# Two key tiles per step in both attention layers of a two-layer transformer kernel

## What is computed

```python
def _layernorm(x, axis=-1, eps=1e-05):
    m = jnp.mean(x, axis=axis, keepdims=True)
    v = jnp.var(x, axis=axis, keepdims=True)
    return (x - m) / jnp.sqrt(v + eps)
...
q_hk = (hidden_q @ Wq.T).reshape(Bv, Sv, H, K)            # H, K = 16, 128
q_big = jnp.einsum('bshk,hkq->bshq', q_hk, w_kc_q)        # layer 0 rotates q_big too
kv_r = _apply_rope(kv_c, sin_k[None], cos_k[None])
q_r = jnp.einsum('bshq,hqr->bhsr', q_big, W_qr)
k_r = jnp.einsum('bld,hdr->bhlr', kv_r, W_kr)
attn = jax.nn.softmax(jnp.einsum('bhsr,bhlr->bhsl', q_r, k_r), axis=-1)
ctx_c = jnp.einsum('bhsl,bld->bhsd', attn, kv_r)
ctx_lat = jnp.einsum('bhsd,hkd->bhsk', ctx_c, w_kc_kv)
return ctx_lat.transpose(0, 2, 1, 3).reshape(Bv, Sv, H * K) @ Wo.T
...
x = x + _L0_xattn_ref(_layernorm(x), ctx_512, ...)
x = x + _L0_ffn_ref(_layernorm(x), ...)                   # 16 experts
x = x + _L1_xattn_ref(_layernorm(x), ctx_512, ...)
x = x + _L1_ffn_ref(_layernorm(x), ...)                   # LoRA experts
```

## Time and profile before

| | us |
|---|---|
| median of 3 runs | 3165.96 (3162.75 to 3173.43) |
| the profiled execution | 3168.89 |
| its span, first to last instruction | 3167.1 |
| layer 0's attention, 192 to 1431 of the span | 1239, PE busy 1142.5 |
| layer 1's attention, 1849 to 2822 | 973, PE busy 938.5 |
| the rest (weights, experts, LoRA experts) | 955, PE busy 772.3 |

### The profile page before, as it was taken

The page is one execution under the profiler, slowest core; times in us unless marked ns, Lnnn a source line. Parts: engine busy times, 40 slices in busy tenths (PEclk is TensorE's granted clock), DMA queues, the critical chain, the costliest instruction groups (busy, mean ns, idle before and its releaser), DMA issues. The chain is left out here.

```text
span 3167.1 us, 42548 instructions
## 1 busy us (share of the span) xinstructions
PE 2853.3 (90%) x15928; PEld 1633.2 (52%) x15928; DVE 1954.6 (62%) x2322; ACT 1177.4 (37%) x1640; POOL 1668.3 (53%) x935
## 2 busy tenths in 40 slices
PE   7689899999998999996899889999999999986898
PEld 6444444444544454443788744444454454445665
DVE  2576667666766676655666556655665655636664
ACT  2124441444144423442333234444443443433331
POOL 0467775776677776771200047677676666742111
PEclk8689999999999999997899989999999999997998
DMA  8333331333133322322000143232323232300000
GB/s 288 109 84 75 87 92 34 88 76 104 36 76 84 92 58 62 75 52 85 1 1 1 28 89 80 66 78 63 75 63 75 63 75 63 83 30 23 7 6 12
DMA packets 98836, 209.15 MB, mean 66 GB/s; under 512 B 30306, under 2 KB 74322, under 8 KB 91116
## 3 DMA queue, kind: packets, MB, share of 16 engines
q1 hardware_dynamic: 98636, 206.44, 25.1%
HBM read 135.36 MB, written 46.00 MB: 57 GB/s over the span
## 5 line engine op out<-in xcount | busy, mean ns | idle before, releaser
L1135 POOL TENSOR_TENSOR sums<-sums,prob 125x896 f32<-125x896 f32 x556 | 1176.1, 2115 | 285.2 <-ACT prob L1075 242.2
L1222 DVE TENSOR_REDUCE maxpart<-pair 112x2 f32<-112x1000 f32 x744 | 889.9, 1196 | 451.8 <-PE pair L937 451.3
L1075 ACT ACTIVATE prob<-wide 125x896 f32<-125x896 f32 x768 | 704.4, 917 | 903.0 <-PE wide L963 901.1
L977 PE MATMUL single<-prob,kv 125*64 125x448 f32 x3072 | 753.8, 569 | 0.5
L958 PE MATMUL wide<-qhigh,kparts 64*125 64x448 f32 x3072 | 448.7, 369 | 1.5 <-DVE maxpart L1222 1.5
L937 PE MATMUL pair<-kparts,qhigh 64*112 64x500 f32 x1488 | 360.7, 481 | 88.0 <-DVE maxpart L1222 86.5
L937 PEld LDWEIGHTS pair<-kparts,qhigh 64*112 64x112 f32 x1488 | 130.1, 171 | 520.6 <-DVE maxpart L1222 440.0
L1135 POOL TENSOR_TENSOR sums<-prob 125x896 f32<-125x896 f32 x64 | 135.1, 2111 | 362.2 <-ACT prob L1075 362.2
L958 PEld LDWEIGHTS wide<-qhigh,kparts 64*125 64x125 f32 x3072 | 281.7, 184 | 79.6 <-issue 48.2
L963 PE MATMUL wide<-shift,ones_row 64*125 64x448 f32 x1536 | 284.5, 365 | 3.9 <-DMA shift<-maxrow 3.9
L958 PE MATMUL wide<-qlow,kparts 64*125 64x448 f32 x1536 | 283.0, 363 | 0.0
(11 more groups left out here) (329 smaller groups left out, 3898.2 us busy)
## 6 DMA issues: line engine op xcount, KB each, us to landing
...
```

Of the source, the lines that this page charges most:

```text
L977: mm = pe.matmul(mix_acc[64 * half:64 * half + DC, 0:HQ], kv[:, b % 3, t, :], prob[:, (b * LT + t) % NPROB, half * HQ:(half + 1) * HQ], st ...
L1075: nc.scalar.activation(prob[:, n_ % NPROB, :].rearrange("p (a b) -> p a b", a=2), acc[0:LP, :, 0:HQ], ACT.Exp)\
L1135: nc.gpsimd.tensor_tensor(dst, first_in, prob[:, n_ % NPROB, :], ALU.add).then_inc(s["pool_sum"], 1)
L1222: V.tensor_reduce(maxpart[:, b % 2, t:NMAX:4, third], acc[0:TQ, :, 0:LB], AX.X, ALU.max).then_inc(*R.signal_drained(kind, *key))
```

## The change

The list is written two tiles at a time. In pair p of a batch (t = 2p) come: maximum t, score t, score t+1, maximum t+1, then mix t-2 and mix t-1, then what falls due. In pair 0 the two mixes are the last ones of the batch before. Other steps move with that:

- `context` of the batch before comes behind pair 0's mixes, so behind both maxima of pair 0; before, it stood ahead of the first of these maxima.
- `spread` (the packed reciprocal) stands in the fourth pair (tiles 6 and 7) instead of tile 8, `share` in the sixth.
- Layer 0: `rope` 0 stands behind the first maximum of pair 1, `rope` 1 behind the second; the three `keyT` end pairs 2, 3 and 4; `ropecos` 0 and 1 stand behind the first maxima of pairs 4 and 5, `rotate` behind the second of pair 4.
- Layer 0, last batch of a group: the two `rstd` stand at the ends of pairs 4 and 5 (before: tiles 7 and 8), `xsplit` at the end of pair 5 (before: tile 9).
- Layer 1: the next group's norm is spread over batches j = 4 and j = 5, with the reciprocal in four pieces (`invert`, 112 columns each) and the products with it in four (`scale`), and the subtraction of `xsplit` in two (`xrest`). Two queries fall in one pair, the first between the maximum and the scores.

```diff
@@ -47,6 +47,8 @@
+NORM_PARTS = (2, 4)
+REST_PARTS = (1, KT)
...
@@ -112,44 +123,60 @@
         maximum(1, i, (PAIR, 0)[i % 2])
     for b in range(NB):
         g, j = divmod(b, BG)
+        following = g + 1 < G
+        for p in range(LT // 2):
+            t = 2 * p
+            queries = following and j == BG - 2 and p < NPAIR // 2
+            if p == 1 and b + 2 < NB:
                 add("fetch", b + 2)
+            ahead(b, t)
+            if queries:
+                add("query", g + 1, t, region=3)
+            if following and j == BG - 4 and p == 3:
+                add("square", g + 1, 0)
+            if following and j == BG - 3 and 1 <= p <= 4:
+                add("scale", g + 1, p - 1)
+            if following and j == BG - 3 and p == 5:
+                add("xrest", g + 1, 0)
+            add("score", b, t, region=0)
+            add("score", b, t + 1, region=1)
+            if b + 1 < NB and p == 4:
                 add("maxneg", b + 1)
+            ahead(b, t + 1)
+            if b + 1 < NB and p == 4:
+                add("maxT", b + 1, region=3)
+            if queries:
+                add("query", g + 1, t + 1, region=3)
+            if p or b:
+                old = (b, t - 2) if p else (b - 1, LT - 2)
+                add("mix", old[0], old[1])
+                add("mix", old[0], old[1] + 1)
+                if not p:
                     add("context", b - 1)
+            if p == 1 and b:
                 add("norm", b - 1, region=3)
+            if g and j == 1 and 2 <= p <= 4:
+                for m, half in (((0, 0),), ((0, 1),), ((1, 0), (1, 1)))[p - 2]:
+                    add("project", g - 1, m, half, region=None if half else 3)
+            if following and j == BG - 4:
+                if p == 2:
                     add("mean", g + 1, region=3)
+                if p == 3:
+                    add("square", g + 1, 1)
+                if p == 5:
                     add("var", g + 1, region=3)
+            if following and j == BG - 3:
+                if p < NORM_PARTS[1]:
+                    add("invert", g + 1, p)
+                if p == 4:
                     add("xsplit", g + 1)
+                if p == 5:
+                    add("xrest", g + 1, 1)
+            if p == 3 and b:
                 add("spread", b - 1)
+            if p == 5 and b:
                 add("share", b - 1, 2)
+    add("mix", NB - 1, LT - 2)
     add("mix", NB - 1, LT - 1)
     add("context", NB - 1)
     add("norm", NB - 1, region=3)
...
@@ -242,59 +270,70 @@
             add("maxT", first, region=3)
             if g:
                 add("attn", g - 1, 3)
-        last = None
         for j in range(BG):
             b = first + j
-            for t in range(LT):
-                ahead = (j + 1, t + EARLY_MAX) if t + EARLY_MAX < LT else (j + 2, t + EARLY_MAX - LT)
-                if layer == 0 and b == 0 and t == 0:
+            for p in range(LT // 2):
+                t = 2 * p
+
+                def ahead(tile):
+                    n = tile + EARLY_MAX
+                    batch, n = (j + 1, n) if n < LT else (j + 2, n - LT)
+                    if batch < BG:
+                        maximum(first + batch, n)
+
+                if b == 0 and p == 0:
                     add("rotate", 2)
                     for part in range(2):
                         add("ropecos", 2, part)
-                if layer == 0 and t == LT - 3 and b + 3 < NB:
+                ahead(t)
+                if p == 1 and b + 2 < NB:
+                    add("rope", b + 2, 0)
+                if p >= 4 and b + 3 < NB:
+                    add("ropecos", b + 3, p - 4)
+                if g + 1 < G and j == BG - 1 and p in (2, 3):
+                    add("square", g + 1, p - 2)
+                add("score", b, t, region=0)
+                add("score", b, t + 1, region=1)
+                if j + 1 < BG and p == 4:
+                    add("maxneg", b + 1)
+                ahead(t + 1)
+                if j + 1 < BG and p == 4:
+                    add("maxT", b + 1, region=3)
+                if p == 4 and b + 3 < NB:
                     add("rotate", b + 3)
-                add("score", b, t, region=t % 2)
-                if j + 1 < BG and t == 8:
-                    add("maxneg", b + 1)
-                if last is not None:
-                    add("mix", *last)
-                    if last[1] == LT - 1:
-                        add("context", last[0])
-                last = (b, t)
-                if t == 1 and j:
-                    add("norm", b - 1, region=3)
-                if j + 1 < BG and t == 9:
-                    add("maxT", b + 1, region=3)
-                if layer == 0 and t in (3, 4, 5) and b + 2 < NB:
-                    add("keyT", b + 2, t - 3, region=3)
-                if layer == 0 and t == LT - 1 and b + 2 < NB:
+                if j or p:
+                    old = (b, t - 2) if p else (b - 1, LT - 2)
+                    add("mix", old[0], old[1])
+                    add("mix", old[0], old[1] + 1)
+                    if not p:
+                        add("context", b - 1)
+                if p == 1:
+                    if j:
+                        add("norm", b - 1, region=3)
+                    if b + 2 < NB:
+                        add("rope", b + 2, 1)
+                if p in (2, 3, 4) and b + 2 < NB:
+                    add("keyT", b + 2, p - 2, region=3)
+                if p == 5 and b + 2 < NB:
                     add("stash", b + 2)
-                if ahead[0] < BG:
-                    maximum(first + ahead[0], ahead[1])
-                if t == 8 and j:
+                if p == 3 and j:
                     add("spread", b - 1)
-                if t == 10 and j:
+                if p == 5 and j:
                     add("share", b - 1, 2)
-                if layer == 0 and t >= LT - 2 and b + 3 < NB:
-                    add("ropecos", b + 3, t - LT + 2)
-                if layer == 0 and t in (1, 2) and b + 2 < NB:
-                    add("rope", b + 2, t - 1)
-                if g + 1 < G and j == BG - 2 and t == 4:
+                if g + 1 < G and j == BG - 2 and p == 2:
                     add("heads", g + 1)
                 if g + 1 < G and j == BG - 1:
-                    if t == 2:
+                    if p == 1:
                         add("mean", g + 1, region=3)
-                    if t in (3, 4):
-                        add("square", g + 1, t - 3)
-                    if t == 5:
+                    if p == 3:
                         add("var", g + 1, region=3)
-                    if t in (7, 8):
-                        add("rstd", g + 1, t - 7)
-                    if t == 9:
+                    if p in (4, 5):
+                        add("rstd", g + 1, p - 4)
+                    if p == 5:
                         add("xsplit", g + 1)
-                    if t == 10:
                         for n in range(SPLIT_AHEAD):
                             add("wsplit", g + 1, n)
+    add("mix", NB - 1, LT - 2)
     add("mix", NB - 1, LT - 1)
     add("context", NB - 1)
     add("norm", NB - 1, region=3)
...
+                elif kind == "invert":
+                    g, part = key
+                    cols = slice(part * NT // norm_parts, (part + 1) * NT // norm_parts)
+                    dve.wait_ge(*R.drained("var", g))
+                    V.reciprocal(x_rstd[:, cols], x_std[:, cols]).then_inc(s["rstd"], 1)
+                elif kind == "scale":
+                    g, part = key
+                    cols = slice(part * NT // norm_parts, (part + 1) * NT // norm_parts)
+                    dve.wait_ge(s["rstd"], norm_parts * g + part + 1)
+                    V.tensor_tensor(x_n[:, :, cols], x_cen[:, :, cols], x_rstd[:, cols].unsqueeze(1).broadcast_to([128, KT, NT // norm_parts]), ALU.mult)\
+                        .then_inc(s["normed"], 1)
+                elif kind == "xrest":
+                    g, k = key
+                    dve.wait_ge(s["x_high"], g + 1)
+                    V.tensor_tensor(x_low[:, k, :], x_n[:, k, :], x_high[:, k, :].bitcast(F32), ALU.subtract).then_inc(s["x_low"], 1)
+                elif kind == "xsplit" and layer == 0:
```

54 lines of the change are left out of this document (17 added, 37 removed).

## The result

The changed kernel takes 3115.77 us (3114.37 to 3117.37, four runs) against 3164.36 for the kernel before in the same comparison: a ratio of 0.984 (95% interval 0.982 to 0.986). The forecast was 3163 with a range down to 3118.

A forecast was written before the change was run, and what follows sets the result against it. PE was taken to set the time wherever nobody makes it wait, with DVE's two-input operations and POOL's additions excluding each other. Layer 0's +36 and layer 1's -39 gave -3 us, so 3163 us against the 3166.0 median; range 3118 to 3187.

The forecast's parts named there:

- (1) *Two tiles per step: Per pair of tiles on PE: 3.90 us against 4.25, by saving one round trip of tile shapes.
- (3) *context: Behind pair 0's maxima, DVE's context waits for POOL's first addition; maximum b of pair 1 starts 1.7 us late.
- context first: Rival, chance 0.05: if POOL's first addition came 0.3 us later, context would cost nothing; 3075 us.
- (4) *keyT: Layer 0, ends of pairs 2 to 4: DVE's subtraction ahead of reduction a costs 0.65 us each, three times.
- (5) *ropecos 0: Layer 0, pair 4: ropecos 0 waits for POOL's addition 7, delaying maxneg; PE waits 1.0 us at maxT (0.4 to 2.3).
- the clock: Rival, chance 0.04: new waits bring a 1.2 GHz stretch in every batch, 64 x 1.7 = 109 us more; 3272 us.
- (6) *ropecos 1: Layer 0, pair 5: POOL's addition 10 is first by 0.08 us, so the next pair starts 1.5 us late.
- ropecos 1 first: Rival, chance 0.27: DVE gets ahead of POOL's addition 10, so 1.5 us falls away in 23 batches; 3128 us.
- The eighth batch: Layer 0, with the query stage: x_low ends about 7 us after PE's last mix; net +3 us (0 to +7).
- Layer 0's +36: Layer 0's total in us: 3 x (7.4 + 3), and +5 in the last group.
- layer 1's sum: Layer 1: eight batches take 239.3 us against 249.3, four times: -39; a regular batch 24.3 + 1.7 = 26.0.
- ctx_n late: Rival, chance 0.14: layer 1's ctx_n misses the gap, waits for addition 10, delays maximum b by 1.9 us; 3175 or 3187.

## Why the prediction was wrong, step by step

The prediction was wrong: the time lies 47 us below it and just outside the range. Of the signs of being wrong that it named, one came: a two-input operation, context, no longer ends behind POOL's addition.

(1) *Two tiles per step*: right. Pairs take 3.93 for 3.90, and a batch of layer 1 without waits 24.5 for 24.3.

(3) *context* is the step that failed. "POOL's first addition starts at 3.27, context is due at 3.57" was read well; "it holds the port until 5.38; context ends at 6.33" did not happen. The start of two records was taken as the order at the port, from rope additions that had met POOL in mid addition. In these runs DVE comes first behind a reduction as if its claim counted from the reduction's start, here 0.76 ahead of the addition. So the term of 1.7 in 52 batches, 88 us, fell away. That is the rival *context first*, with the right price and the wrong condition: the addition came no later than forecast. Its chance, 0.05, hung on that condition. "SBUF — State Buffer" of the Trainium skill ("SBUF: two separate sides") says that whichever operation starts first gets the pair. The trace agrees as it stands where DVE was idle (ctx_n at 1111.73); behind a reduction it agrees only if DVE's start is put at that of the reduction.

(4) *keyT*: right, 0.64 for 0.65, three times a batch.

(5) *ropecos 0* was mis-sized: 1.0 forecast, 2.0 measured, near the bound of 2.3. POOL had not drifted to where the sum put it; the addition is caught 0.86 after its start. A little of it is the sum's own: from 2.34, four additions at 2.24 and a rotation of 1.95, with 2.1 for the last addition, end at 13.1 and not at 12.95. And the wait brought what the sum did not hold: the half-clock stretch. With it, it is 8.1 to 8.3 from the second exponential of pair 4 to the first of pair 5 (19 regular batches), in the three that lose the port without it 6.5 to 6.7, in the one in which ropecos 0 had the port 4.8. So ropecos 0 behind an addition costs 1.8, and the clock 1.7; over 19 regular batches the clock makes 32 us. The prediction priced a stretch at 1.7 too, but as a rival with a chance of 0.04 that needed all 64 batches. "TensorE: Matmul & The Clock Gate" of the Trainium skill ("A second HAM failure mode") says of another kernel that frequent short idles make the clock oscillate. Layer 0 now has 122 us at 1.2 GHz in 26 stretches, 19 of them behind this wait, so the trace leans to the page.

(6) *ropecos 1* was half right: in some two thirds of the regular batches it is 5.1 to 5.2 from the last exponential to the next batch's first, in the others 3.2 to 3.7, a difference of 1.5 to 2.0 for the 1.5 forecast. *ropecos 1 first* is thus no case of its own; it happens batch by batch.

The eighth batch was mis-sized: +8.4 for +3. x_low ended some 7 after PE's last mix, as forecast, but the last link of the chain is the weights' low part, another 0.9 and a product's start later, and PE's wait at var did not go.

Layer 0's +36 was therefore right only in sum: context's 1.7 a batch less, the clock, maxT and the eighth batch more. Its regular batches of 31.5 and 33.4 lie around the forecast 32.4. Layer 1 has neither ropecos nor keyT, so there the failed step stood nearly alone: its batches without norm, queries or project took 24.5 for 26.0, and the layer came out 44 us below its forecast, nearly the whole miss. (Two slips in layer 1's sum, 24.3 + 8 x 1.5 is 36.3 and four times 10.0 is 40, are worth some 3 us and decide nothing.)

*ctx_n late* and *the clock* as cases of their own did not occur in the form given.
